# A first rank written out with deeper order, the tally inside it, and sorts spread between messages, in a two-layer graph kernel on one core

## The reference

```python
h = jnp.maximum(_layernorm(x, axis=-1), 0.0)
# layer 0: weighted sum of h[src] over the edges of each dst, then linear, plus a linear map of h
agg = segment_sum(h[src] * edge_weight[:, None], dst, num_segments=N)
x = x + (agg @ W_neigh + b_neigh + h @ W_self.T)
h = jnp.maximum(_layernorm(x, axis=-1), 0.0)
# layer 1: its edge part doesn't read h; row = src
s, m = segment_sum(edge_attr, row), segment_max(edge_attr, row)      # m is 0 where a node has no edge
mean = s / maximum(count, 1)
h1 = relu(concatenate([s, m, mean, u[batch]], 1) @ W1 + b1)
x = x + (h1 @ W2 + b2)
```

## Time and profile before

| | |
|---|---|
| median of 3 runs | 2242.63 us (2241.53 to 2242.85) |
| the profiled execution | 2241.82 us, of which 2240.1 are its span |
| mean granted TensorE clock | 0.641 |
| VectorE busy | 1617.5 us (72%) |
| TensorE busy (products / weight loads) | 1258.9 us (56%) / 1073.5 us (48%) |
| GpSimd busy | 1101.9 us (49%) |
| ScalarE busy | 494.4 us (22%) |
| indirect DMAs on GpSimd | 391 of 987 ns (gathers), 391 of 1000 ns (scatters) |

### The profile page before, as it was taken

One profiled execution on the slowest core, in us unless ns is written; L12 is line 12 of the kernel. 1 busy time (PEld: TensorE's weight loads), 2 busy tenths in 40 slices (PEclk: granted clock), 3 DMA queues, 4 the chain that ended last, 5 costly groups with the idle time before them and its releaser, 6 DMA issues. The chain is left out here.

```text
span 2240.1 us, 41882 instructions
## 1 busy us (share of the span) xinstructions
PE 1258.9 (56%) x14884; PEld 1073.5 (48%) x14885; DVE 1617.5 (72%) x3568; ACT 494.4 (22%) x888; POOL 1101.9 (49%) x1404
## 2 busy tenths in 40 slices
PE   4566565400001444433277777777777777777775
PEld 3444443300000333322266666667676666666665
DVE  5766767810068888766488888888888888888886
ACT  1221211100000211111132333333332333333332
POOL 7777777777773777777222222222222222232220
PEclk7565555555555555555577777777777777777776
DMA  9700000100063222222545555555555555555551
GB/s 263 95 13 13 12 13 13 55 28 13 13 154 82 76 76 79 73 61 67 104 109 122 125 119 120 125 123 121 124 119 123 123 118 124 118 123 126 119 123 32
DMA packets 405256, 203.62 MB, mean 91 GB/s; under 512 B 370375, under 2 KB 377799, under 8 KB 404407
## 3 DMA queue, kind: packets, MB, share of 16 engines
q1 hardware_dynamic: 254792, 93.02, 19.4%
q0 software_dynamic: 46976, 72.79, 14.3%
q10 hardware_dynamic: 103312, 35.54, 6.3%
HBM read 138.46 MB, written 62.73 MB: 90 GB/s over the span
## 5 line engine op out<-in xcount | busy, mean ns | idle before, releaser
L592 POOL DMA_INDIRECT xg_all<-in_x_dram,idx_src x391 | 385.9, 987 | 149.4 <-issue 118.3
L598 POOL DMA_INDIRECT by_win<-rows,idx_win x391 | 391.2, 1000 | 127.3 <-issue 127.3
L969 POOL DMA_DIRECT2D rows<-by_win x98 | 52.2, 532 | 782.4 <-DVE arena L1000 753.7
L1110 PE MATMUL ps<-arena,w1r 32*128 32x192 f32 x2352 | 214.2, 526 | 267.8 <-DVE arena L1000 264.6
L1110 PEld LDWEIGHTS ps<-arena,w1r 32*128 32x128 f32 x2352 | 164.6, 302 | 280.1 <-DVE arena L1000 276.6
L974 POOL DMA_DIRECT2D rows<-flag_d x392 | 214.4, 554 | 13.7 <-issue 13.6
L1122 PE MATMUL ps<-w_sb,arena 128*96 128x64 f32 x1568 | 185.8, 285 | 0.0
L1122 PEld LDWEIGHTS ps<-w_sb,arena 128*96 128x96 f32 x1568 | 184.4, 203 | 0.0
L1197 ACT ACTIVATE arena<-ps,hbias 128x768 f32<-128x768 f32 x98 | 88.3, 901 | 413.0 <-PE ps L1110 413.0
L417 ACT ACTIVATE sq<-xc 128x512 f32<-128x512 f32 x147 | 91.6, 623 | 364.7 <-DVE xc L399 364.7
L427 PE MATMUL ps<-ident,h 128*128 128x128 f32 x196 | 54.6, 434 | 174.4 <-DVE h L412 174.4
(11 more groups left out here) (191 smaller groups left out, 2840.9 us busy)
## 6 DMA issues: line engine op xcount, KB each, us to landing
rows<-message SPq DMA_DIRECT2D x784, 36.4 KB, 2.0
rows<-flag_d POOLq DMA_DIRECT2D x392, 72.0 KB, 2.6
rows<-in_x_dram SPq DMA_DIRECT2D x97, 256.0 KB, 3.1
out_dram<-rows ACTq DMA_DIRECT2D x97, 256.0 KB, 2.8
message<-m_row SPq DMA_DIRECT2D x48, 388.0 KB, 2.3
zeros<-slot_d POOLq DMA_DIRECT2D x98, 144.0 KB, 2.9
by_win<-zeros ACTq DMA_DIRECT2D x12, 808.5 KB, 10.6
arena<-by_win SPq DMA_DIRECT2D x7, 1386.0 KB, 9.4
```

Source lines behind the costliest of these rows:

```text
L592: nc.gpsimd.indirect_dma_start(out=xg[g % RX][:, t % GT, :], out_offset=None, in_=x, in_offset=bass.IndirectOffsetOnAxis(ap=idx_src[:, t:t ...
L598: nc.gpsimd.indirect_dma_start(out=by_win, out_offset=bass.IndirectOffsetOnAxis(ap=idx_win[0:parts, t:t + 1], axis=0), in_=rows[0:parts, t ...
L1110: last = nc.tensor.matmul(ps[z_bank[q]][:, 0:2 * SL], w1r[DE * q:DE * q + DE, j, :], part[DE * q:DE * q + DE, :], start=(j == 0), stop=(j ...
```

## The change

The rank of src becomes a function of its own, written out without a loop over 49 groups (`place_dve`, `place_pe`, `place_act`). The one-hots are made two groups ahead in three buffers, the arithmetic on places (`place`) comes one group behind, and four tiles share one product where the tables allow it: a group has 30 matmuls (2 and 8 for the comparison, 8 for the histogram, 2 transposes, 8 counts, 2 look-ups) instead of 50. For that, histogram and scan stand on all 128 partitions, in four copies. The one-hots of dst and the tally, now 2 products a group, go inside this rank and out of `message_of`; so do the totals behind it. dst is loaded ahead of the attributes. The sorts come one at a time behind messages 9, 14, 19, 24, 29, 34 and 39, and keep(g - 2) stands in message_of(g) where keep(g - 1) stood. The node loop isn't touched.

```diff
+        def place_dve(dve, own, r, hg):
+            def spread(g):
+                one_hots(g, w_hi[g % 3], w_lo[g % 3], "win").then_inc(r["oh"], 1)
+            def tallied(g):
+                if g >= 2:
+                    dve.wait_ge(hg["used"], g - 1)
+                one_hots(g, t_hi[g % 2], t_lo[g % 2], "dst").then_inc(hg["oh"], 1)
+            def same_of(g):
...
+            def chain(g):
+                b = g % 2
+                dve.wait_ge(r["w"], g + 1)
+                own(nc.vector.tensor_copy(hist_all[b][:, :, 0], begin_all[1 - b][:, :, GT]))
+                own(nc.vector.tensor_tensor_scan(
+                    begin_all[b][:, :, :].rearrange("p l k -> p (l k)"), chain_mask[:, :, :].rearrange("p l k -> p (l k)"),
+                    hist_all[b][:, :, :].rearrange("p l k -> p (l k)"), 0.0, ALU.mult, ALU.add))
+                if g >= 2:
+                    dve.wait_ge(r["look"], g - 1)
+                nc.vector.tensor_tensor(begin4[b][:, :, :].rearrange("p m (q l) -> p (m q) l", l=DIGIT),
+                                        begin_all[b][:, :, 0:GT].rearrange("p l k -> p k l"),
+                                        lane_of[:, :, :].rearrange("p m q -> p (m q)").unsqueeze(2).to_broadcast([P, GT, DIGIT]),
+                                        ALU.mult).then_inc(r["begin"], 1)
+            spread(0)
+            spread(1)
+            for g in range(MG):
+                chain(g)
+                same_of(g)
+                if g >= 1:
+                    place(g - 1)
+                if g + 2 < MG:
+                    spread(g + 2)
+                tallied(g)
+            place(MG - 1)
...
+        def place_pe(pe, r, hg):
...
+            first(0)
+            for g in range(MG):
+                if g + 1 < MG:
+                    first(g + 1)
+                second(g)
+                if g >= 1:
+                    tally(g - 1)
+            tally(MG - 1)
+        def place_act(act, r):
+            for g in range(MG):
+                b = g % 2
+                act.wait_ge(r["h"], g + 1)
+                if g >= 2:
+                    act.wait_ge(r["begin"], g - 1)
+                for q in range(4):
+                    last = nc.scalar.activation(hist_all[b][DIGIT * q:DIGIT * q + DIGIT, :, 1:GT + 1],
+                                                h_ps.rearrange("p k l -> p l k"), ACT.Copy)
+                last.then_inc(r["w"], 1)
+                act.wait_ge(r["t"], g + 1)
+                if g >= 2:
+                    act.wait_ge(r["look"], g - 1)
+                nc.scalar.activation(ohT4[b], t4_ps, ACT.Copy).then_inc(r["ohT"], 1)
...
+        SORT_AT = [EARLY + 1 + 5 * n for n in range(NB)]
...
                 edge_load(sp, src_i, src, "src")
+                edge_load(sp, dst_i, dst, "edges")
...
+                sp.wait_ge(made["starts"], 1)
+                sp.dma_start(starts_d[0, :].rearrange("(p l) -> p l", p=DIGIT), start_i["dst"][:, :]).then_inc(starts_out, 16)
+                sp.wait_ge(starts_out, 16)
+                sp.dma_start(starts[:, :, :], starts_d.unsqueeze(0)).then_inc(loaded["starts"], 16)
-                for g in range(EARLY):
+                for g in range(SORT_AT[0] - 1):
                     store(g)
                 sp.wait_ge(win_sent, 16 * (FT + 1))
                 take(0)
                 take(1)
+                for g in range(SORT_AT[0], MG + 2):
+                    if g >= SORT_AT[0] + 1:
+                        store(g - 2)
+                    if g in SORT_AT:
+                        n = SORT_AT.index(g)
+                        sp.wait_ge(srt["sorted"], n + 1)
...
+                own(nc.gpsimd.memset(lane_of[:, :, :], 1.0))
+                own(nc.gpsimd.affine_select(out=lane_of[:, :, :], in_=lane_of[:, :, :], compare_op=ALU.is_ge, fill=0.0,
+                                            base=0, pattern=[[0, 2], [-DIGIT, 4]], channel_multiplier=1))
+                own(nc.gpsimd.affine_select(out=lane_of[:, :, :], in_=lane_of[:, :, :], compare_op=ALU.is_ge, fill=0.0,
+                                            base=DIGIT - 1, pattern=[[0, 2], [DIGIT, 4]], channel_multiplier=-1))
...
                     norm_centre(own, b, xg[r])
-                    dve.wait_ge(hg["used"], g + 1)
-                    one_hots(g, b, "dst").then_inc(hg["oh"], 1)
                     norm_sum(dve, b, g + 1)
-                    if g not in (0, EARLY):
-                        keep(g - 1)
+                    if g >= 2:
+                        keep(g - 2)
                     norm_scale(dve, own, b, g + 1, ew[:, g * GT:g * GT + GT]).then_inc(msg["h"], 1)
...
-                for g in range(EARLY):
-                    message_of(g)
-                keep(EARLY - 1)
                 dve.wait_ge(loaded["counts"], 16 * NB)
                 own(nc.vector.tensor_scalar(win_ok[:, :], win_n[:, :], float(SL), None, ALU.is_le))
-                for n in range(NB):
-                    sort_batch(n)
-                for g in range(EARLY, MG):
+                for g in range(MG):
                     message_of(g)
+                    if g in SORT_AT:
+                        sort_batch(SORT_AT.index(g))
+                keep(MG - 2)
                 keep(MG - 1)
```

More of the change, by code:

```diff
@@ L442, in evacuate_hT @@
             nc.scalar.activation(hT[b][:, :, :], ps[bank][:, :].rearrange("p (k c) -> p k c", c=P), ACT.Copy).then_inc(done, 1)
-        loaded = {n: sem(f"loaded_{n}") for n in ("weights", "src", "edges", "attr", "starts", "counts", "keys")}
+        loaded = {n: sem(f"loaded_{n}") for n in ("weights", "src", "edges", "weight", "next", "attr", "starts", "counts", "keys")}
         made = {n: sem(f"made_{n}") for n in ("const", "pads", "wsT_ps", "wsT", "c0_ps", "hbias", "c0", "srcs", "rows",
-                                              "counts", "starts", "messages", "zeros")}
+                                              "counts", "starts", "messages", "zeros", "falls")}
         starts_out, counts_out = sem("starts_out"), sem("counts_out")
@@ L529, in _ @@
                 take(1)
-                for n in range(NB):
[L531 to L535, removed]
-                for g in range(EARLY, MG):
[L537 to L541, removed]
+                for g in range(SORT_AT[0], MG + 2):
[4 more added lines that the diff above has]
+                        sp.wait_ge(srt["sorted"], n + 1)
+                        sp.dma_start(slot_d[n * SB:n * SB + SB, :], slots[n % 2][:, :]).then_inc(order_out[n % 2], 16)
+                        sp.dma_start(flag_d[:, n * SB:n * SB + SB, :].rearrange("f w c -> w f c"), flags[n % 2][:, :, :]).then_inc(order_out[n % 2], 16)
+                        if n + 2 < NB:
+                            take(n + 2)
                 for b in range(2):
@@ L647, in _ @@
                     own(nc.vector.memset(flags[b][:, 0, 0:1], 0.0))
-                own(nc.vector.memset(start0["win"][:, :], 0.0))
                 dve.wait_ge(loaded["src"], 32)
@@ L686, in _ @@
                 dve.sem_inc(made["c0"], 1)
+                dve.wait_ge(loaded["weight"], 16 * 2)
                 def message_of(g):
@@ L780, in _ @@
                 pe.wait_ge(made["const"], 1)
-                rank_pe(pe, r_win)
-                pe.wait_ge(r_win["done"], NG + 2)
-                pe.wait_ge(r_win["t_used"], NG + 1)
-                pe.wait_ge(r_win["h_used"], NG + 1)
+                place_pe(pe, r_win, hg)
+                pe.wait_ge(hg["rows"], 1)
+                nc.tensor.matmul(ps[6][0:DIGIT, 0:1], before[0:DIGIT, :], row_total[:, :], start=True, stop=True)
+                nc.tensor.matmul(ps[4][0:DIGIT, 0:1], ones[:, 0:DIGIT], falls[:, :],
+                                 start=True, stop=True).then_inc(hg["base"], 1)
                 pe.wait_ge(loaded["weights"], 16 * 15)
```

185 lines of the change are left out of this document (128 added, 57 removed).

## The result

The changed kernel takes 2201.93 us (median of 4 runs, 2200.36 to 2204.1) against 2242.74 for the kernel before in the same sitting: a ratio of 0.9818 [0.9801, 0.9835], 41 us faster. The forecast had the sign and missed the size: 2215.5, range 2207 to 2228. The profiled execution is 2200.36 us, its span 2198.6; the mean granted clock is 0.641, as before.

The account below looks back on a forecast made before the run. GpSimd's queue of 782 indirect DMAs was taken to bound the stage before an unchanged node loop. Terms -28.65 + 4.5 - 3.0 = -27.15 from 2241.82, plus 0.8 to the median: 2215.5 us, range 2207 to 2228.

Parts of the forecast that it names:

- The ring's wait: GpSimd's 28.95 us stop before a gather, whose buffer waits for VectorE's xc behind all seven sorts; spreading them: -28.65 us.
- The message behind: A message VectorE makes while behind the gathers, not waiting for their data: 7.69 us was to become 6.75.
- The rank had slack: VectorE's rank, 6.5 us a group forecast, stays covered by eight scatters' 10.6 us, so a faster rank gains nothing itself.
- Rival 1: Spread sorts leave VectorE ever further behind the gathers, giving the gain back: 2241 us, no change; chance 0.06.
- What VectorE costs GpSimd: +4.5: Stretching of GpSimd's scatters and gathers beside VectorE's two-input work, priced at 0.18 us per us: +4.5 us together.
- the part ahead of the gathers: Scatters beside the rank, stretched by 0.14 us more a group from added two-input work: +6.5 us.
- the gathers, -2 forecast: Gathers beside the messages, stretched less with one-hots gone and some 34 messages behind, 7 in step: 2 us less.
- rival 3: Each us of added two-input work fully blocks GpSimd beside the scatters, +38: 2249 us, slower; chance 0.04.
- Rival 2's far end: One-hots, not xc, stretch gathers, and VectorE's new rank order falls between scatters, -10 more: 2205 us; chance 0.05.
- The tail: Block end before the node loop: totals and start positions move behind the rank, off SP's last path: -3 us.
- The node loop: The last 1147 us, from 1093 us on, untouched by the diff and expected to keep its length: 0.
- The upper bound of the stretching: Each pair of one-hots in the rank costs GpSimd 0.30 us, 49 times: +15 us.

Follow-up runs that it names:

- spread only: Kernel before the change with only the seven sorts spread behind messages 9, 14, ... 39: 2214.99 us undisturbed, ratio 0.9874 to the kernel before.
- all in PSUM: Changed kernel with the mean, the scale of h and the split's remainder in PSUM: 2179.82 us undisturbed, ratio 0.9729 to the kernel before.
- mean in PSUM: Changed kernel with a message group's mean kept in PSUM, so xc reads one operand from SBUF: 2195.83 us undisturbed, ratio 0.9789 to the kernel before.
- more one-hots: Changed kernel with the dst one-hots made twice in each rank group: 2209.28 us undisturbed, ratio 0.9867 to the kernel before.
- longer rank: Changed kernel with an extra, unused single-input reduction of 0.42 us in each rank group: 2204.26 us undisturbed, ratio 0.9832 to the kernel before.
- Late flag: Changed kernel with GpSimd waiting for the last message row before it reads the totals' flag: 2207.18 us undisturbed, ratio 0.9841 to the kernel before.
- centre later: Changed kernel with a small unused reduction ahead of xc in each message: 2466.88 us, ratio 0.9409 to the kernel before, in a disturbed sitting only.

## Why the prediction was right about the sign and wrong about the size

**What held.** The ring's wait: 28.65 forecast, gone; spread only alone is worth 28 us. The message behind: 6.75 forecast, 6.75 measured (660.13 to 666.88), with VectorE waiting 0.69 us for the square, as the prediction had it, and not for TensorE. From the key load to the first sort 10.85 us against 10.4; the sort began at 640 and not at 660, 14 us of that because the scatters had ended so much earlier. Five messages and a sort took 47.5 us (653.44 to 700.91), as forecast. The rank had slack, 5.75 us a group where 6.5 was forecast (no scatter waited for it by more than 0.9 us in all). Rival 1 (the gain given back) fell: no gather waited. VectorE had caught up with the gathers by message 23, at 770.70, long before the end, so 26 of the 41 messages were made behind and 15 waited for their data, where the prediction had 34 and 7.

**The step that failed: "What VectorE costs GpSimd: +4.5".** It priced the stretching in proportion to the two-input work, 0.18 us of GpSimd for each us. Both of its parts came out with the wrong sign: the part ahead of the gathers, +6.5 forecast, gave 14.2 back, and the gathers, -2 forecast, paid 6.2. The work itself grew by more than forecast (the product at L323 takes 0.61 us and not 0.42), so at that price the term would have been larger still. On the gathers, a message made behind was to cost 0.16 us and cost 0.47. The price is not per us of work. This is a scatter of the kernel before, on its timeline:

```profile
204.07 0.75 DVE L293 TENSOR_TENSOR_SCAN begin<-chain_mask,hist 32x288 f32<-32x288 f32 x1
...
204.33 1.26 POOL L598 DMA_INDIRECT by_win<-rows,idx_win  x1 [0.30 <-issue]
...
205.79 0.45 DVE L299 TENSOR_TENSOR begin_p<-begin,begin_p 32x288 bf16<-32x288 f32 x1
205.90 1.19 POOL L598 DMA_INDIRECT by_win<-rows,idx_win  x1 [0.30 <-issue]
...
211.18 0.96 POOL L598 DMA_INDIRECT by_win<-rows,idx_win  x1 [0.30 <-issue]
211.63 0.75 DVE L293 TENSOR_TENSOR_SCAN begin<-chain_mask,hist 32x288 f32<-32x288 f32 x1
...
212.45 1.16 POOL L598 DMA_INDIRECT by_win<-rows,idx_win  x1 [0.30 <-issue]
```

The scatter begins 0.26 us after the scan and 0.49 us before its end, and takes 0.30 more than the 0.96 of an unhindered one; the next begins 0.11 after the subtraction, 0.34 before its end, and takes 0.23 more. It is held until the VectorE instruction has some 0.12 to 0.19 us to go. In the changed kernel at 205.81 scan and scatter start together, and the scatter takes 0.96: the scan's 0.78 us beside it cost nothing. The next one, at 207.07, starts when the product of 206.63 (the subtraction's heir, L323) has 0.16 us to go, and takes 0.96 too. Of the 34 scans that begin in 97:297, 16 begin 0.007 to 0.016 us behind a scatter's start and 17 begin 0.65 us ahead of one, with some 0.1 us to go when it starts; none costs anything.

Counts worked out from the timelines, of indirect DMAs that start under a two-input instruction with more than 0.15 us still to go, and of the time by which they are longer than the others:

| | kernel before | changed kernel | all in PSUM |
|---|---|---|---|
| scatters beside the rank | 56 of 210, 13.9 us | 33 of 155, 1.8 us | |
| behind them | scan 19 (6.1), subtraction 19 (4.1), one-hots 18 (3.7) | | |
| gathers | 59 of 327, 11.2 us | 72 of 327, 16.9 us | no such instruction |
| behind them | xc 25 (7.3), third part 25 (3.2) | xc 36 (10.6), third part 36 (6.3) | |

13.9 less 1.8 is the 12.05 us of the scatters. The places can be read from the lengths, and in each kernel they repeat. A rank group of 5.75 us is 4.5 scatters of 1.277, so that each instruction meets the scatters at the same two places in group after group, and these happen to be free. Nothing in the change aimed at them: these 12 us are luck. The old hardware loop repeated as well, but at bad places: its two groups of a trip took 7.56 and 7.07 us, together eleven scatters, and in every trip one scan, one subtraction and one one-hot held a scatter while the other scan (211.63 above) fell between two. A message behind has become 6.75 us, five gathers of 1.25 with the 0.29 and 0.18 by which two of them are stretched (10.6/36 and 6.3/36; 6.72 in all). Each of the 26 messages made behind meets a gather, with xc 0.27 to 0.28 us ahead of it, where in the kernel before a message of 7.69 met one every second time (13 of its 26). That the second SBUF input is what stretches gathers beside xc and h is shown by mean in PSUM (same meeting, no stretching) and all in PSUM (no stretching at all, 22 us). That place and not amount sets the price is shown by the two kernels' ranks (more two-input work, 1.8 us lost instead of 13.9) and by the trace of more one-hots, whose scans, on 128 partitions as in the changed kernel, cost 10.3 us, so that the new rank's instructions aren't harmless in themselves; the longer rank, where only one-input work was added and 3.6 us were lost instead of 1.8, points the same way within the noise. Why the two queues settle just at these places was only argued, and what those 1.8 us would be in another kernel can't be forecast from this.

The Trainium skill, "SBUF — State Buffer", section "Who interferes with whom", says "Issue order, not op shape, decides who blocks". The trace agrees: the same scan costs 0.30 us when it began 0.26 us earlier and nothing when it began 0.007 us later. The same page, in the section "Summary: rules for kernel authors", says that the second one to issue fully blocks, which the prediction took at its word for rival 3, 2249 us; the full block is what one meeting shows, to within 0.12 to 0.19 us of the end, but the sum goes by the number of meetings, and that fell.

**Rival 2's far end** ("VectorE's new rank order falls between scatters, -10 more"), 2205 with a chance of 0.05, is what happened to the scatters: -12.05. Its first half, that the one-hots rather than xc stretch gathers, fell: xc is the first cause.

**The tail: -3 forecast, -8.2 measured.** The path was mis-sized. The prediction let SP's two DMAs or VectorE's arithmetic hold the end; what held it besides was GpSimd's drain of 5.96 us, which began only when the totals' flag had come. From the last store to the first load it was 12.25 us and is 4.0 (1044.12 to 1048.12). Late flag put 7.25 of the 8.2 back without a DMA of SP's moved.

**The node loop: 0 forecast, +3.3 measured.** Its code and its instruction counts are the same, the extra time lies in its first ten groups, and the same loop took 1147.7 us in late flag, 1148.4 in all in PSUM and 1151.2 in spread only. What sets it stays open; nothing was tried on it.

In spans, the miss is -20.7 on the part ahead of the gathers, +8.2 on the gathers, -5.2 on the tail and +3.3 on the node loop: -14.3 together. The upper bound of the stretching, +15, was drawn; the lower, -2, held only that it "doesn't grow". That it could vanish was in the prediction as a rival and should have been the lower bound, since the trace of the kernel before already showed 14.2 us of it.

## What to carry to other kernels

Where a queue of short instructions on one engine is stretched by another engine, don't multiply a mean stretch by the amount of work: list the meetings on the timeline (who started first, by how much) and see whether they repeat from period to period; then bound the term from all of it gone to one hit in every period. The cure that worked here is to take the second SBUF operand away, into PSUM where there is room, from every instruction of the period at once, since with one contender removed the pattern moved to the next. And look at what each engine does between its last instruction and the next block: a flag that comes late to an engine with a slow drain costs the drain too.

## What the runs showed of the hardware that was not expected

An indirect DMA of GpSimd that starts under a running VectorE instruction with two SBUF inputs, a scan, a subtraction, a one-hot or `scalar_tensor_tensor` alike, is held until about 0.12 to 0.19 us before that one's end: 0.95 becomes 1.24 us beside xc. In the undisturbed traces that held only from some 0.045 us behind the instruction's start on; a DMA that began nearer to it lost nothing, save twice, where another one-hot had just run. With one of the two inputs in PSUM it was 0.95 under the same overlap for xc, h and the third part; beside the split's first subtraction, which has one input in PSUM in every kernel, 36 gathers of the changed kernel lost 0.04 us each. A cast with a single SBUF input held a gather too (centre later). GpSimd's drain at the block's end took 5.94 to 5.96 us where it began with nothing of its own under way, the others' 7 to 17 ns. The same node loop took 1147.1 to 1151.2 us in different kernels.
